# Sums by destination cleared on ScalarE, the row mask kept in a buffer of its own, and a bilinear product laid out the other way round

## The reference, cut to what matters

```python
x = ln(x + gnn0(x))                      # edge softmax by destination
# layer 1: a bilinear product of two node vectors, summed by source
messages = einsum('eu,ev,uvw->ew', x[src], x[dst], W_tp)
x = ln(x + zeros.at[src].add(messages) @ weight.T + bias)
# layer 2: two GIN convolutions, each with a sum by destination
agg = segment_sum(x[src], dst); h = relu(relu((1+eps1)*x + agg @ ...) ...)
agg = segment_sum(h[src], dst); x = ln(x + log_softmax(...))
# layer 3: typed messages summed by destination, then a GRU cell
m = segment_sum(einsum('emh,eh->em', emb[type], x[src]), dst)
x = ln(x + gru(m, x))
```

## Time and profile before

| | us |
|---|---|
| median of 3 runs | 5363.5 (5358.63 to 5366.24) |
| the profiled execution, own time | 5358.86 |
| its span in the trace | 5357.0 |
| busy: DVE | 3796.2 (71%) |
| busy: PE | 3260.3 (61%) |
| busy: POOL | 3045.7 (57%) |
| busy: ACT | 1645.2 (31%) |
| bilinear stage | 2448 to 3010 |
| pass 1 of the sums by destination | 3010 to 3543 |
| pass 2 | 3645 to 4178 |
| pass 3 | 4421 to 5057 |

### The profile page before, as it was taken

How to read it: one execution, slowest core, us unless ns; L and a number is a source line. 1 busy time by engine, 2 the same in 40 slices (tenths; PEclk the granted TensorE clock), 3 DMA queues, 4 the chain that set the end, 5 groups by cost and what they waited for, 6 DMA issues and landing times.

```text
span 5357.0 us, 56936 instructions
## 1 busy us (share of the span) xinstructions
PE 3260.3 (61%) x12357; PEld 2396.4 (45%) x12357; DVE 3796.2 (71%) x6342; ACT 1645.2 (31%) x4066; POOL 3045.7 (57%) x2659
## 2 busy tenths in 40 slices
PE   5888888888805344436878444453444544766686
PEld 2444444444405334435767334443344324666432
DVE  5999999999966555536999755644556674555588
ACT  2555555555532111102333101111111341222143
POOL 2666666666612888885555677715777007776000
PEclk9999999999995665558999655676556565666598
DMA  3111111111142444431211000041000320000122
GB/s 93 36 44 42 38 44 41 41 41 44 27 111 53 57 58 62 59 40 36 55 41 51 14 7 7 7 116 35 7 7 7 103 86 10 7 7 7 35 82 75
DMA packets 400935, 231.46 MB, mean 43 GB/s; under 512 B 127626, under 2 KB 365646, under 8 KB 400802
## 3 DMA queue, kind: packets, MB, share of 16 engines
q1 hardware_dynamic: 281522, 210.43, 13.8%
q0 software_dynamic: 119296, 19.68, 6.8%
HBM read 152.10 MB, written 58.54 MB: 39 GB/s over the span
## 4 chain that ended last, share of the span: by engine, by line
POOL 34%; DVE 26%; issue 19%; PE 9%; DMA 6%; ACT 2%; SPq 2%; DVEq 1%; POOLq 0%; ACTq 0%
POOL extra L667 21%; POOL sums L652 9%; DVE arena L1599 4%; POOL xg L630 3%; DMA sums<-cmb,sidx 3%; DVE arena L1323 2%; DVE arena L1347 2%; PE ps L1127 2%; PE ps L994 2%; DMA edge_in<-far_row 2%; POOL ft_t L619 1%; PE ps L1085 1%; DVE arena L1543 1%; DVE ps L1317 1%; DVE arena L1331 1%
## 5 line engine op out<-in xcount | busy, mean ns | idle before, releaser
L1085 PE MATMUL ps<-arena 128*128 128x128 f32 x2976 | 687.0, 424 | 764.2 <-DVE arena L1526 692.7
L667 POOL DMA_INDIRECT extra<-x_t,srci x784 | 780.1, 995 | 527.0 <-issue 527.0
L1085 PEld LDWEIGHTS ps<-arena 128*128 128x128 f32 x2976 | 638.3, 326 | 804.9 <-issue 804.9
L652 POOL DMA_INDIRECT sums<-cmb,sidx x392 | 613.6, 1565 | 336.4 <-ACT cmb L781 204.3
L994 PE MATMUL ps<-edge_in,wl 17*128 17x512 f32 x784 | 704.4, 1076 | 87.3 <-DMA edge_in<-far_row 85.1
L1543 DVE TENSOR_TENSOR arena<-arena,ps 128x128 f32 x1488 | 427.8, 287 | 368.3 <-PE ps L1085 193.1
L630 POOL DMA_INDIRECT xg<-in_x,xidx x392 | 437.5, 1116 | 353.1 <-DVE xp L1305 233.4
L619 POOL DMA_INDIRECT ft_t<-fts,fidx x392 | 506.7, 1293 | 139.2 <-issue 117.6
L1032 PE MATMUL ps<-arena 128*128 128x128 f32 x992 | 226.8, 421 | 521.1 <-DVE arena L1410 521.1
L667 POOL DMA_INDIRECT extra<-h_t,srci x392 | 383.4, 978 | 251.5 <-issue 251.5
L832 ACT ACTIVATE ps<-extra 128x16 f32 x1488 | 171.3, 168 | 1066.1 <-SPq L583 868.6
(11 more groups left out here) (200 smaller groups left out, 5978.9 us busy)
## 6 DMA issues: line engine op xcount, KB each, us to landing
edge_in<-far_row SPq DMA_DIRECT2D x98, 256.0 KB
ain<-in_src_row SPq DMA_DIRECT2D x56, 448.0 KB, 3.9
sums<-zero SPq DMA_DIRECT2D x132, 144.0 KB
ain<-arena SPq DMA_DIRECT2D x42, 448.0 KB, 5.2
arena<-rel_t SPq DMA_DIRECT2D x63, 256.0 KB, 4.0
x_t<-yout SPq DMA_DIRECT2D x28, 448.0 KB, 3.3
extra<-x_t,srci POOLq DMA_INDIRECT x784, 2.4
xin<-x_t SPq DMA_DIRECT2D x28, 448.0 KB, 4.7
```

The source lines that it names most:

```text
L652: pool.indirect_dma_start(sums[k], bass.IndirectOffsetOnAxis(ap=sidx[n % 2][:, j:j + 1], axis=0), cmb[n % 2][:, j, :], None, compute_op=AL ...
L667: pool.indirect_dma_start(dy[:, t, :], None, table, bass.IndirectOffsetOnAxis(ap=srci[:, t:t + 1], axis=0)).then_inc(d_gathered[n % QUEUE] ...
L1085: last = pe.matmul(ps[2][:, j * P:(j + 1) * P], oneh[b][:, j * P:(j + 1) * P], placed[b][:, j * P:(j + 1) * P], start=True, stop=True)
```

## The change

`acc` is cleared by ACT instead of DVE: 14 copies of the zero tile (128x896) and one of 128x128, after the last `yout` of the node stage before, ahead of ACT's first pick. DVE's clear and DVE's mask at the head of each pass are gone; `jmask` has its own buffer and is made once, at L1569. In the bilinear stage the order of the 256 products of a slot becomes (w, u), with the summed u innermost: `wb` is made in that order, `multiply` repeats x over the middle dimension, and the reduce reads its inputs without a step.

```diff
-        jmask = edge_in.bitcast(BF16)[:, 0:SLOT_GROUPS * SG * PACK]
+        jmask = sb("jmask", [P, SLOT_GROUPS * SG * PACK], BF16)
...
-            return eng.tensor_tensor(o.rearrange("p (s u w) -> p s u w", s=2, u=F),
-                                     products.rearrange("p (s u w) -> p s u w", s=2, u=F),
-                                     x_tile.rearrange("p (k f) -> p k f", f=F)[:, s0:s0 + 2, :].unsqueeze(3)
+            return eng.tensor_tensor(o.rearrange("p (s w u) -> p s w u", s=2, u=F),
+                                     products.rearrange("p (s w u) -> p s w u", s=2, u=F),
+                                     x_tile.rearrange("p (k f) -> p k f", f=F)[:, s0:s0 + 2, :].unsqueeze(2)
                                      .broadcast_to((P, 2, F, F)), ALU.mult)
...
                 act.activation(io_p, io_8[:, :], ACT.Copy).then_inc(io_done, 1)
+                act.wait_ge(y_done, node_count(k + 2, 0, 0))
+                for t in range(NODE_TILES):
+                    act.activation(acc[:, t * W:(t + 1) * W], zero[:, :], ACT.Copy)
+                act.activation(acc[:, NODE_TILES * W:(BLOCKS + 1) * P], zero[:, 0:(BLOCKS + 1) * P - NODE_TILES * W],
+                               ACT.Copy).then_inc(acc_done, ACC_ZEROS)
...
-                dve.tensor_scalar(o, ps[0][:, 0:256], blk[:, j:j + 1], None, ALU.mult).then_inc(w_made, 1)
+                dve.tensor_scalar(o.rearrange("p (w u) -> p w u", u=F),
+                                  ps[0][:, 0:256].rearrange("p (u w) -> p w u", u=F), blk[:, j:j + 1], None,
+                                  ALU.mult).then_inc(w_made, 1)
...
-                if k == 0:
-                    dve.wait_ge(slots_done, 3)
-                dve.memset(acc, 0.0).then_inc(acc_done, ACC_ZEROS)
-                n_slots = SLOT_GROUPS * SG
-                dve.tensor_tensor(jmask.rearrange("p (s j) -> p s j", j=PACK), iota.broadcast_to((P, n_slots, PACK)),
-                                  relj[:, 0:n_slots].unsqueeze(2).broadcast_to((P, n_slots, PACK)),
-                                  ALU.is_equal).then_inc(mask_done, 1)
-                dve.wait_ge(mask_done, k + 2)
                 dve.wait_ge(io_done, k + 1)
...
-                                      ([prod[n_par(c, g)]] + pool_prod)[k].rearrange("p (s u w) -> p s w u", s=2, u=F),
+                                      ([prod[n_par(c, g)]] + pool_prod)[k].rearrange("p (s w u) -> p s w u", s=2, u=F),
```

## The result

The changed kernel has a median of 5244.3 us (5242.26 to 5249.11, 4 runs), against 5361.1 of the kernel before beside it (5354.73 to 5366.24, 4 runs). The ratio is 0.9783, with a 95% interval of 0.9771 to 0.9794. Forecast were 5232, with a range from 5205 to 5278. The gain is 117 us where 131 were forecast. The profiled execution took 5246.19 us, with a span of 5244.4.

A forecast was written before the change was run, and what follows sets the result against it. No single engine bounds the program; DVE bounds the bilinear stage, and POOL's gathers pace the destination sums. Bilinear gain 91 us plus 40.3 from first gathers: 5363.5 - 131 = 5232 us, range 5205 to 5278.

The forecast's parts named there:

- The reduce: Bilinear stage, L1599: without the step, 685 ns instead of 1016, so 0.33 us less for each of 28 a tile.
- PE sets the pace of packs 4 to 6: Bilinear stage: PE at 4.13 us a pack becomes the bound there; DVE sets the pace only around the norm.
- The period, 32.9: Bilinear stage, one tile: 14.1 + 0.6 + 18.2 = 32.9 us instead of 39.56, worth 87 us over 13 periods.
- DVE's stretch: Bilinear tile, DVE from L394 of pack 0 to that of pack 3: 18.2 us instead of 22.2, by 12 shorter reduces.
- ends ahead of the L394 of pack 3 even at 5.96: Bilinear stage: PE's pack 2, even at part clock (5.96 us), ends before DVE's L394 of pack 3.
- First and last tile: Bilinear stage, outside the 13 periods: the first tile gains 2.6 us, the last 1.2, having no next pack to wait for.
- POOL's product at 1058: Bilinear stage, POOL's L394: stays at 1058 ns with the new layout of x, hidden up to about 1.35 us.
- The first gather: Head of each destination-sum pass, L667: without DVE's clear and mask, 0.97 us like the second, instead of 14.40.
- The rival on a fixed cost: Head of a pass: the first gather's 14.40 us is a fixed starting cost, leaving only the bilinear gain, 5272 us; 8%.
- another cause: Head of a pass: by the skill's rule the memset couldn't hold the gather, so its 14.40 us would come from elsewhere.
- 13.43 us a pass: Sums by destination: all later gathers and the tail come 13.43 us earlier in each of three passes, 40.3 us together.
- ACT's clears covered: Head of a pass: ACT's clears take at most 13.6 us and end before its first pick, with 1.5 us to spare.

The follow-up runs named there:

- e5: Changed kernel, but POOL's products alone read x the old way, repeated on the innermost dimension: 5265.4 us, ratio 0.9792 to the kernel before.
- e3: Changed kernel with the clear of `acc` back on DVE, still no mask at the head of a pass: 5264.8 us, ratio 0.9795.
- e9: e3 with only the instruction queued behind DVE's memset changed in each pass: 6328 us in a slower call (kernel before there: 6438).
- e2: Kernel before with only the clear on ACT and the mask's own buffer, old product layout: 5340.8 us, ratio 0.9932.
- e1: Kernel before with only the new product layout; clear and mask stay on DVE: 5305.6 us, ratio 0.9865.
- e6: Changed kernel with pass 3's type mask in PSUM, so that L1508 reads one SBUF input: 5223.8 us, ratio 0.9733.
- e7: Changed kernel with the next tile's pack 1 moved ahead around the bilinear norm (DVE's L394, ACT's pack work): 5236.3 us, ratio 0.976.
- e10: e6 and e7 together, plus pack 2's L394 and ACT's copy of turned pack 3 moved ahead: 6336.1 us in a slower call, ratio 0.9838.

## Why the prediction was right or wrong

- **The reduce**: 685 ns forecast, 674 measured. The line laid through the reduces of neighbours held. Right.
- **PE sets the pace of packs 4 to 6**: right, with 4.12 us a pack at full clock. DVE is idle 73.5 us for PE's banks, against 40.8 before.
- **The period, 32.9**: measured 33.89 between the same points. This is the mis-sized term: (39.57 - 33.89) x 13 = 74 us instead of 87, nearly all of the 14 us. The chain is the one that was laid out, and three of its four terms were too small. DVE's stretch: 18.2 forecast, 18.56 measured (18.44 at the median, and one bias of 3.71 us). From L394 of pack 3 to PE's pack 4: 0.82 forecast, 1.15 measured. Packs 4 to 6 with the wait for loads: 13.0 forecast, 12.86 measured. From PE's start of pack 0 to DVE's L394 on its first bank: 0.9 forecast, 1.31 measured. The second comes from the step "ends ahead of the L394 of pack 3 even at 5.96". That sentence is true (2632.19 against 2635.41) but asks the wrong question. PE's pack 3 follows the slow pack and starts at 2632.69, so pack 4 can't start before 2636.81, while I had it start 0.82 behind L394, at 2636.23. It happens in six tiles; in the other seven L394 comes last and the 0.82 holds. The last is 3.62/4 for a bank, taken from PE's rows, and in the kernel before DVE never waited for that bank from the second tile on. That the granted clock would come nearer 1 was right (0.95 and 1.00 in the two tiles above).
- **First and last tile**: the first gained 2.7 (2.6 forecast). The last gained nothing; I had 1.2.
- **POOL's product at 1058**: wrong, 1272 at the median. e5 shows the cause, the layout of x. The median stayed below the 1.35 from which I had it decide, the mean of all 294 (1381 ns) didn't. With it back at 1057, in e5, PE's stretch is no shorter (15.44 against 15.33), so it wasn't what the period lacked.
- **The first gather**: 1.02 and 0.94 us, as forecast. The rival on a fixed cost fell. But "what held it" was only half read: I took both instructions together. e3 and e9 show that the memset alone holds nothing, so moving the clear to ACT brought nothing in passes 1 and 2; it mattered only in pass 3, where L1499 stands behind it. The Trainium skill's rule that I had set against my sum (SBUF — State Buffer, "Who interferes with whom") was right on the memset (gathers of 0.94 to 1.02 us beside it in e3), and the conclusion that I drew from it, "another cause", was right too: the cause is what is queued behind the memset, in the kernel before the mask.
- **13.43 us a pass**: 14.7 and 16.4 in passes 1 and 2 (13.1 and 13.7 in e2). I can't say where the 1 to 3 us more come from. In pass 3 only 3.1: the head gave 13.4, and nine more gathers met an L1508, about 1 us each. How many meet one is chance: e1, e2, e3 and e5, with another timing ahead of the pass, have 38 to 45 where after has 21. With as many, after would have taken some 20 us more (an estimate at 1 us a gather), and the forecast would have been 32 us off instead of 12. I had read such a collision in the softmax, and didn't ask where else a DVE instruction with two SBUF inputs stands beside gathers. e6 prices the whole of it: 23 us in after.
- **ACT's clears covered**: right, with 3.20 us to spare at the pick.

## What to carry to other kernels

When a gather looks long, look at the DVE instruction beside it, and, where that is a memset, *at the one queued behind it*. If it has two inputs in SBUF, put one of them into PSUM (e6), or run it ahead of the memset (e9). A gain of 13 us in one place can be lost to such collisions in another, so count the long gathers of every pass after a change.

When a bound moves, cut the period into stretches by who waits for whom, and add up the rows of each stretch alone. An engine's hole or slow piece counts only if nothing else is waited for behind it: in after the tiles with the slow pack were no longer than those without. And an order moved for one engine changes what lies beside what: e7 took 0.6 us out of DVE's stretch, and e10 put them back with one instruction of 56 elements beside POOL's product.

## What the runs showed of the hardware that was not expected

- A DVE instruction of 0.16 us with two SBUF inputs, queued behind a memset of 10.62 us, held a POOL gather for 10.35 us; one with one SBUF input and a constant didn't (0.95), and neither did one with two SBUF inputs behind a product with an input in PSUM (0.94, e6 and e3).
- A gather beside a running DVE product with two SBUF inputs took 1.97 instead of 0.94 us; with one input in PSUM, never over 1.02. Gathers that started up to 0.04 us behind the product escaped.
- POOL's product of 128x512 floats took 1057 ns with x repeated on the innermost dimension, 1272 with it repeated on the middle one. DVE's took 679 and 683.
- DVE's product of 56 elements with constants (L1400) took 0.19 us at the least, and 1.09 in the mean of e5's bilinear stage, beside POOL's products.
